# Moving the copy of turned q, and the next batch's row powers, inside the projection stages of a fused top-k, attention and GRU kernel

## The reference

```python
def _rms_norm(x, g):
    y = xf * jax.lax.rsqrt(jnp.mean(xf * xf, axis=-1, keepdims=True) + EPS)
    return y.astype(x.dtype) * g
...
xn = _rms_norm(x, g_norm) * (1.0 + scale) + shift
qkv = xn @ W_qkv
qkv = qkv.reshape(b, n, 3, h, d)
q, k, v = jnp.moveaxis(qkv, 2, 0)
...
q = _rms_norm(q, g_q)
k = _rms_norm(k, g_k)
logits = jnp.einsum('bhqd,bhkd->bhqk', q, k) * d ** (-0.5)
attn = jax.nn.softmax(logits, axis=-1)
o = jnp.einsum('bhqk,bhkd->bhqd', attn, v)
o = jnp.swapaxes(o, 1, 2).reshape(b, n, dim)
return o + o @ W_out
```

## Time and profile before

| | |
|---|---|
| Median of 3 runs | 2241.61 us (2240.93 to 2247.2) |
| The profiled execution, its own time | 2243.18 us |
| Its span from first to last instruction | 2241.5 us |
| TensorE matmul busy | 2132.2 us (95%) |
| VectorE busy | 1638.1 us (73%) |
| ScalarE busy | 1290.9 us (58%) |
| GpSimd busy | 529.6 us (24%) |
| Projection stages with their tail, batches 0 to 3 | about 160 to 216, 294 to 362, 441 to 509, 587 to 652 us |

### The profile page before, as it was taken

One profiled execution on the slowest core, in us unless ns is written; L12 is line 12 of the kernel. 1 busy time (PEld: TensorE's weight loads), 2 busy tenths in 40 slices (PEclk: granted clock), 3 DMA queues, 4 the chain that ended last, 5 costly groups with the idle time before them and its releaser, 6 DMA issues.

```text
span 2241.5 us, 135672 instructions
## 1 busy us (share of the span) xinstructions
PE 2132.2 (95%) x57232; PEld 1833.4 (82%) x57232; DVE 1638.1 (73%) x6269; ACT 1290.9 (58%) x5763; POOL 529.6 (24%) x2255
## 2 busy tenths in 40 slices
PE   5768999999999999999999999999999999999998
PEld 3654555645545899999999999999999999999997
DVE  7988977878788587777677766667766666767665
ACT  6765946748668345555556655545555544555543
POOL 2002120031210222332233222222222222222221
PEclk8559999999999999999999999999999999999999
DMA  5000000010010000000000000000000000000000
GB/s 209 3 2 1 1 1 1 1 57 1 1 57 2 22 5 5 4 1 1 1 1 1 1 10 1 1 11 0 1 11 1 1 1 10 1 1 11 13 9 14
DMA packets 8410, 26.49 MB, mean 12 GB/s; under 512 B 1028, under 2 KB 1352, under 8 KB 7880
## 3 DMA queue, kind: packets, MB, share of 16 engines
q1 hardware_dynamic: 7712, 23.07, 2.7%
q10 hardware_dynamic: 424, 0.07, 0.0%
HBM read 18.94 MB, written 4.19 MB: 10 GB/s over the span
## 4 chain that ended last, share of the span: by engine, by line
PE 80%; DVE 14%; ACT 3%; issue 3%; DMA 1%; POOL 0%; SPq 0%; DVEq 0%; POOLq 0%; ACTq 0%
PE psum L2264 54%; PE psum L2225 8%; PE psum L2008 3%; PE psum L2026 2%; PE psum L1971 2%; PE psum L1992 2%; PE psum L2110 2%; PE psum L1928 2%; DVE region_cols L1232 2%; DVE region_cols L1248 2%; DVE top L1426 2%; ACT region_rows L786 1%; PE psum L1948 1%; DMA region_cols<-in_L_cond_W_emb_dram 1%; PE psum L1902 1%
## 5 line engine op out<-in xcount | busy, mean ns | idle before, releaser
L2264 PE MATMUL psum<-partsA,region_w_hh 128*128 128x40 f16 x24576 | 855.4, 179 | 10.4 <-issue 4.4
L2264 PE MATMUL psum<-partsB,region_w_hh 128*128 128x40 f16 x24576 | 853.4, 179 | 0.1
L2264 PEld LDWEIGHTS psum<-partsA,region_w_hh 128*128 128x128 f16 x24576 | 759.0, 96 | 36.6 <-DVE partsA L1762 11.4
L2264 PEld LDWEIGHTS psum<-partsB,region_w_hh 128*128 128x128 f16 x24576 | 724.4, 96 | 0.7 <-issue 0.2
L599 POOL TENSOR_TENSOR region_w_b<-region_w_b 128x16 f32<-128x16 f32 x1022 | 243.6, 238 | 1079.8 <-DVE region_w_b L1751 1079.8
L1725 DVE TENSOR_REDUCE psum<-psum 128x8 f32<-128x32 f32 x1024 | 201.5, 197 | 199.7 <-PE psum L2264 188.9
L1061 ACT ACTIVATE mixA<-psum 128x8 f32<-128x8 f32 x512 | 94.6, 185 | 428.9 <-DVE psum L1725 428.8
L1075 ACT ACTIVATE region_w_b<-psum 128x8 f32<-128x8 f32 x1024 | 188.9, 184 | 145.2 <-DVE psum L1740 87.3
L601 POOL COPY region_work<-region_w_b 128x8 f32<-128x8 f32 x1024 | 229.5, 224 | 2.2 <-DVE region_w_b L1751 2.2
L1751 DVE TENSOR_TENSOR_SCAN region_w_b<-giveB,region_w_b 128x40 f32<-128x40 f32 x512 | 123.6, 241 | 128.5 <-ACT region_w_b L1075 128.5
L1732 DVE TENSOR_REDUCE psum<-psum 128x8 f32<-128x32 f32 x1024 | 190.9, 186 | 0.4 <-PE psum L2264 0.2
(11 more groups left out here) (265 smaller groups left out, 2837.4 us busy)
## 6 DMA issues: line engine op xcount, KB each, us to landing
region_rows<-in_x_dram SPq DMA_DIRECT2D x4, 1024.0 KB, 11.0
region_w_a<-in_L_cond_W_qkv_dram SPq DMA_DIRECT2D x1, 3072.0 KB, 23.4
region_w_hh<-in_L_cond_W_hh_dram SPq DMA_DIRECT2D x4, 768.0 KB, 7.0
region_w_a<-in_L_cond_W_ih_dram SPq DMA_DIRECT2D x1, 3072.0 KB, 9.8
out_dram<-region_w_b SPq DMA_DIRECT2D x12, 256.0 KB, 2.2
region_cols<-in_L_cond_W_emb_dram SPq DMA_DIRECT2D x1, 2048.0 KB, 19.5
region_cond<-in_cond_dram SPq DMA_DIRECT2D x1, 1024.0 KB, 10.9
region_w_a<-in_L_cond_W_out_dram SPq DMA_DIRECT2D x1, 1024.0 KB, 21.5
```

The costliest lines, as they stand in the source:

```text
L2264: made = e.matmul(k.slots(bank)[:, :, ch, :, 0:2], k.w16[:, 2 * read + c, part, NC * "rzn".index(g) + 2 * half + ch], k.parts[read][:, c]. ...
```

## The change

In both loops the copy of turned q of tile t - 1 moves up, into the middle of the take of tile t. On ScalarE it now stands between the squares of tile t and the root of tile t; on VectorE between the scaled sum (L1365) and the reciprocal (L1367). The next batch's row powers move from tile 1 to tile 2, its row root and row scales from tile 2 to tile 3. Nothing is added or removed, and the orders of TensorE, GpSimd and the queues stay. The line numbers of the new kernel are 10 to 12 higher in the lines concerned.

```diff
 def act_take_projected(e, k, b, t):
+    act_squares(e, k, b, t)
+    if t:
+        act_turn_stack(e, k, b, t - 1, 0)
+    act_head_roots(e, k, b, t)
+
+
+def act_squares(e, k, b, t):
     s = k.sem
...
         e.activation(k.qk[:, t, i * HEADS:(i + 1) * HEADS], k.bank(bank, HEADS, DH), ACT.Copy).then_inc(s["qk_rows"], 1)
-    e.wait_ge(s["head_power"], 3 * n + 2)
+
+
+def act_head_roots(e, k, b, t):
+    s = k.sem
+    e.wait_ge(s["head_power"], 3 * (NT * b + t) + 2)
     e.activation(k.head_power[:, t], k.head_power[:, t], ACT.Sqrt).then_inc(s["head_root"], 1)
...
         act_take_projected(e, k, b, t)
-        act_turn_stack(e, k, b, t - 1, 0)
         if b == B - 1:
             for c in WEIGHT_CHUNKS[t]:
                 act_high_weights(e, k, c)
-        elif t == 1:
+        elif t == 2:
             act_row_powers(e, k, b + 1)
-        elif t == 2:
+        elif t == 3:
             act_row_roots(e, k, b + 1)
...
     e.tensor_scalar(k.head_power[:, t], k.head_power[:, t], 1.0 / DH, EPS, ALU.mult, ALU.add).then_inc(s["head_power"], 1)
+    if t:
+        dve_turn_stack(e, k, b, t - 1, 0)
     e.wait_ge(s["head_root"], n + 1)
     e.reciprocal(k.head_power[:, t], k.head_power[:, t]).then_inc(s["head_power"], 1)
     dve_norm_heads(e, k, b, t)
...
         dve_take_projected(e, k, b, t)
-        dve_turn_stack(e, k, b, t - 1, 0)
         if b == B - 1:
             for c in WEIGHT_CHUNKS[t]:
                 dve_low_weights(e, k, c)
-        elif t == 2:
+        elif t == 3:
             dve_row_scales(e, k, b + 1)
```

## The result

| | before | after |
|---|---|---|
| Median of 5 runs each | 2243.10 us (2240.93 to 2247.20) | 2232.07 us (2230.36 to 2233.53) |
| Ratio, with its 95% interval | | 0.9947 (0.9934 to 0.9960) |
| The profiled execution, its own time | 2243.18 us | 2233.17 us |
| Its span | 2241.5 us | 2231.4 us |

The kernel became 0.5% faster. The forecast was 2230.2 us in a range of 2227 to 2238, with 0.79 on faster by over 0.3%.

What follows compares the result with a forecast made beforehand. TensorE held 80% of the chain, so only its standstills in the four projection stages counted, chiefly waits for copies of turned q. 4.3 + 4.9 + 0.6 + 1.6 = 11.4 us off the median 2241.61 gave 2230.2 us, range 2227 to 2238.

Steps and rivals of the forecast that it cites:

- Batches 1 and 2, the wait: Second half of turned k of tile 0 starts 2.86 us earlier in each batch, with some 0.8 us idle left.
- The clock: Behind the shorter gap TensorE's clock does not fall: 1.70 us gained in batch 1, 1.90 + 0.41 in batch 2.
- rival 1: The clock falls all the same behind the gap in batches 1 and 2; 2233.7 us, chance 0.14.
- Late next: q transposes of tile 1, batches 1 and 2: copy of turned k does not move, so TensorE waits 0.27 us.
- rival 2: New wait at q transposes of tiles 1 and 2, from ScalarE's row powers or GpSimd's gains; 2236.6 us, chance 0.11.
- Batch 3: Copy's place does not matter but fills 0.27 us VectorE waited for the root; two tiles by 0.3, 0.6 us gained.
- Batch 0: Second half of k of tile 0 can start 2.1 us earlier; 1.6 us gain taken, bounds 0 and 2.1.
- one of my signs of being wrong: Idle time over 0.5 us before the q transposes of tile 1 or 2 would show the forecast wrong.
- Rivals 3 and 4: ScalarE held by its waiting copy, kernel slower, 2255, chance 0.05; stage end hangs on another chain, no difference, 2241, 0.06.
- the later root: Root waits for copy of turned q: in tile 2 the copy is done first, in tile 3 0.4 us, inside the covers.
- The cover: Batches 1 and 2, slack before TensorE arrives: about 2.5 us in tile 2, 4 us in tile 3; cost 0.

## Why the prediction was right, and where not

**Batches 1 and 2, the wait: right.** From the mark to the second half of k of tile 0 it was 19.52 us before (324.33 - 304.81) and is 16.64 (318.26 - 301.62): 2.88 us, forecast 2.86. In batch 2 it is 2.86. The idle time left is 0.90 and 0.92 us, forecast "some 0.8". Each copy alone shows that VectorE's is the one that counts.

**The clock: right in both terms, for this pair of executions.** The granted clock is 1.00 all the way, so rival 1 fell. The terms were 1.70 and 1.90 + 0.41 us. In batch 1 the sixteen records' stretch was 8.62 us before (324.78 to 333.40); it is 7.34 now, of which 0.42 is the wait at its end, hence 1.70. But I had drawn the margin too much as a matter of the gap's length: the run with VectorE's copy alone early fell in one batch and held in the other after the same 2.0 us. After gaps of about 1 us, where the rows of before had held, it held here in batches 1 and 2 too. That is no rule either: with the row powers put back it fell in batch 3 after 0.55 and 1.18 us still. And the term is no fixed gain: 31 of 71 executions of the kernel before kept a mean clock of 0.970 or more, and the changed kernel is only 6.9 us ahead of these. The stages gained 9.1 us together; without the two clock terms, 1.70 and 2.32, that is 5.1. The forecast took the clock terms from one execution that had the falls and set them against a median, 2241.61 us, that lies between the two groups, and I did not see that choice.

**Late next: the step that was mis-sized in batches 1 and 2.** That the copy of turned k "does not move" failed in size. Against the mark it ended 24.86 us in before (329.67 - 304.81) and now ends at 25.30. I took 0.27 us of waiting at q of tile 1 and it is 0.91: 0.42 ahead of the first half, and 0.49 between the first half and the next product (1.39 instead of 0.90). So 2.88 + 1.70 - 0.91 = 3.67 us, and in batch 2 2.86 + 2.32 - 0.91 = 4.27. The cause is named in rival 2 ("GpSimd's part may slip because VectorE's low parts now run beside its sums"), and I gave it no price in the forecast. VectorE's low parts of q began 1.8 us earlier against the mark (19.37 for 21.20), fell among the sums and gains, and both became longer: 3.46 us for 1.79, 1.71 us for 1.27. The gains' 0.44 us are most of the 0.64 missed. Nearly all the rest is my arrival time: I let the products begin at the end of the second half, 0.62 us after its start, and in the timeline they begin 0.45 us after it (324.33 to 324.78 before, 318.26 to 318.71 after), so TensorE is there 0.17 us earlier and waits as much longer. Moving the sums away shows that the wait hangs on them: in tile 2 they leave no wait, and the batches take 52.04 and 52.06 us.

**Batch 3: the step that failed.** "The copy's place in that chain does not matter, but it now fills the 0.27 us": the copy does fill time in which VectorE had waited for the root, and more than I took, some 0.4 us. But its place did matter. Reading PSUM, it had kept VectorE busy until GpSimd's gains were nearly through. Without it the low weights cost 0.60 us more. Net that is 0.20 us more per tile where I had forecast 0.3 less, and 0.34 us for the stage. This is shown: the distances are longer in all four runs of the table with the early copy, and as before in the three others. The other 0.28 us of the +0.62 are the later start of the gains of tile 0 in this execution, which no run ties to the change. That +0.62 us is near what two tiles would give by the 0.27 us of the forecast, 2 x (0.60 - 0.27) = 0.66, is chance.

The Trainium skill (SBUF — State Buffer, section on the two separate sides) says that VectorE, for an instruction with two SBUF inputs, and GpSimd, for one that reads SBUF, share a pair of ports as an exclusive lock for a whole instruction, while ScalarE and TensorE wait for nobody. The rows agree as far as they go: low parts and low weights, which have two SBUF inputs, become longer beside GpSimd's adds and gains, GpSimd's too, while ScalarE's squares and stacks beside its adds keep their 0.60 and 1.06 us. I had read the 1.11 us of the scaled sum as its length; beside no GpSimd work it is 0.18. The scaled sum has one SBUF input, so that the sentence drawn on does not cover it; in the trace it ends 0.03 us after GpSimd's first add, 317.60 and 317.57 us, and 320.80 and 320.77 before. It looks like a wait for that add, and no run here shows more.

**Batch 0: right, by 0.2 us.** The second half of k of tile 0 no longer waits; at q of tile 1 TensorE waits 0.59 and 0.32 us. Over 0.5 us there was one of my signs of being wrong; it stands in batch 0 and, with 1.18 and 1.19 us, in batch 3, and in batches 1 and 2 it is 0.25 and 0.32 us. That the row powers' move belongs to the gain only together with the copies was not in my working.

**Rivals 3 and 4.** ScalarE's copy does stand behind a wait for the transposes in tile 3 of batch 1, 2.49 us, as rival 3 has it; the copy ends at 340.41 and the root at 340.53, and TensorE has no wait up to the scores. I had taken 0.4 us for the later root there, and that was wrong: the scaled sum ends at 337.88 and the root begins at 340.31, 2.4 us later. The cover held, as did the one of tile 2. Rival 3 shows in small where the row powers move without the copies.

**What no step had.** TensorE's clock fell in the profiled execution of before at the start of batch 0's attention, and did not after the change. That is 0.92 us in favour of the change, and it is chance: the same changed kernel, profiled once more, has the fall. One microsecond there in the kernel before, the changed kernel, and the changed kernel once more:

```profile
220.00:221.00 1.00, 1.00 (x6) 0.98 (x5) 0.74 (x1) 0.90 (x4) 0.00 (x0) 0.50 0.00 0
...
220.00:221.00 1.00, 0.78 (x6) 0.33 (x4) 1.00 (x2) 1.00 (x4) 0.19 (x1) 1.00 0.00 0
...
220.00:221.00 1.00, 1.00 (x6) 0.86 (x5) 0.51 (x1) 1.00 (x3) 0.19 (x1) 0.50 0.00 0
```

This attention took 88.86, 87.94 and 88.66 us in the three. In all thirteen profiled executions it took 88.6 to 88.9 us where the clock fell in it, and 87.9 to 88.0 where it did not.

The 0.51 us ahead of the first mark and the +0.4 behind the stages lie outside the change too. From batch 3's scores to the end the changed kernel took 1590.1 us in one execution and 1587.8 in the other. Left out, the stages make 9.1 us of the 11.4 forecast; that the time came within 2 us of the forecast is in part luck.

## What to carry to other kernels

Before an instruction of VectorE is moved earlier, look at what GpSimd does at its new time and what it had kept apart: here a copy from PSUM, as a spacer, kept 0.6 us a tile off VectorE's low weights (0.2 us of it was left after what the early copy saved), and GpSimd's adds in a covered tile instead of the tight one were worth 1.8 us a batch. When the wait on top is taken away, work out the chain below it with the lengths that it will have at its new time, not those that it had. And where TensorE stands still for 2 us or more, the same wait can cost 1.7 us more or nothing more, as the clock falls or holds (55.74 and 54.08 us above); that alone is a reason to shorten it. Last, a stage that matches its forecast to 0.01 us proves nothing while the same order takes 0.6 us longer in another execution: split the stage at marks that only the change can move.

## What the runs showed of the hardware

- The same instruction of VectorE, 128 x 32 fp32 from and to SBUF (the scaled sum), takes 0.18 us with GpSimd still and 1.11 or 1.23 us beside its adds of 128 x 512; a pair of 128 x 512 with one fp16 input takes 1.29 and 3.42; a pair of 128 x 1536 3.59, 4.18 or 5.19. VectorE's copies from PSUM keep their 0.68 us beside the same adds.
- GpSimd pays too: its multiplication by the gains takes 1.27 or 1.71 us, four adds 5.92 or 8.86.
- TensorE's clock, at 2.4 GHz before, fell to 1.2 GHz after 2.02 us still in one batch and held after 2.03 us in another of the same execution. After 3.52 us still the transposes ran at 2.4 GHz in one kernel (0.62 us) and at 1.2 GHz in another (1.04 us). It held after 1.10 and 1.24 us with 0.61 us of transposes between, and fell after 0.55 and 1.18 us with 0.62 us between. After 3.79 us in one piece it was at 1.2 GHz from the first transpose on, after 2.02 and 1.60 us with transposes between it fell only some way into the products.
- In one and the same kernel the clock fell at the start of batch 0's attention in one execution (88.66 us) and held in another (87.94 us). The kernel before had a mean granted clock of 0.965 to 0.972 over 71 executions, and took 2247.2 us at the one end and 2237.0 us (median of three) at the other.
- After GpSimd's `partition_all_reduce` at the start of batch 3's stage, its next instruction, the gains of tile 0, began 2.0 to 3.1 us after the multiplication that it needed had ended (12.87 us), and the start moves from execution to execution.
